# Normalising three of four token groups ahead, inside the stage before, in a one-core Trainium2 kernel of eight layers

## The chip, the cores and the metric

The kernel runs on one core of one Trainium2 chip. The time is device microseconds (us) of one execution, the median of several. The profiled execution is one of its own, and its span runs from the first to the last instruction of the core.

## The reference

2048 tokens (2 sequences of 1024) of 256 numbers pass four layers, each an attention and a feed-forward part with a residual, gated by tanh of an input. Nearly every part begins with the same layer norm over the 256 numbers of a token:

```
def _layernorm(x, axis=-1, eps=1e-05):
    m = jnp.mean(x, axis=axis, keepdims=True)
    v = jnp.var(x, axis=axis, keepdims=True)
    return (x - m) / jnp.sqrt(v + eps)
```

The parts, in order: joint attention (L0x), an 8-expert feed-forward (L0f), cross attention on 154 context tokens with a second norm of its own, with gain and shift (L1x), a routed feed-forward with 16 experts and 2 shared (L1f), linear attention (L2x), two local transformer layers (L2a0, L2f0, L2a1, L2f1), a feed-forward whose weights are the context (L3c) and a quantised feed-forward (L3f).

## The kernel before, in words

The tokens lie in SBUF as `x[128 partitions, T=16 tiles, 256]`. Four tiles are a group (G=4 groups, GT=4 tiles, GN=512 tokens). Stages are written as blocks: each engine (TensorE `tensor`, VectorE `vector`, ScalarE `scalar`, GpSimd `gpsimd`, SyncE `sync`) has its own list of instructions, ordered by semaphores, and all meet at a block's end; `net.reclaim()` clears semaphores and adds a barrier. `Weights(..)` with `load` is a block of its own in which SyncE issues the transfer; `w.need()` is another, in which SyncE waits until it has landed.

The norm between two stages is the block `layer_norm`. VectorE writes variance plus eps (L142 or L144), ScalarE takes the root (L174), VectorE the reciprocal (L147) and minus mean times reciprocal (L149), and the 16 tiles are normalised into `xn`: 13 by VectorE (L152), 3 by ScalarE (L170); with no transposed output it is 8 and 8. TensorE transposes them into 8 PSUM banks, four 128x128 blocks each (L163), and ScalarE alone brings the banks into `xT` (L189, or L191 with gain and shift). The mean and variance come from the stage before: `RowStats.take` does `bn_stats` (L96) for some tiles and then `bn_aggr` (L99). `root_table` (L104) loads ScalarE's table for the root early.

The norms that matter here, by the time of their first instruction: 681 us (inside cross attention, after its block of keys and values), 987 us (into L1f), 1343 us (into L2x), 1435 us (into the local layers, output by token, no transposes) and 2241 us (into L3c). Those at 12, 533 and 2293 us are left as they are.

Around them:

- The block of keys and values of `cross_attention`. GpSimd issues 16 gathers (indirect DMAs, L1720) that add the experts' results to `x`, then computes the rest of `wq` (L211) and `gated_bias` (L1725). VectorE evicts keys and values (value items 2, 3, 6 and 7 are the tails, four copies each, L1741), computes the rest of `wo` (L211, 128x2048, both operands in SBUF), and takes the statistics of a group once its gathers have landed.
- The main block of `cross_attention`. After its last unit TensorE projects group 3, VectorE adds it to `x` (L2023), then takes the last two statistics.
- `feed_forward`, for L1f and L2f1. Units `i = g*U + u`; TensorE does `up(i+2)`, then `down_mm(i)`. ScalarE applies the activation (L356) and splits weights three units ahead (L341); VectorE forms the hidden values (L432, L440, L429) and splits them (L206, L211); GpSimd computes the weights' rest. At `u == 0` of the next group VectorE runs `take(g-1)`: adds the result to `x` (L403, for L2f1 also L415) and takes the group's statistics. `up(i+2)` waits for `act_done` and `banks_read` of unit i, `down_mm(i)` for `hidden_ready`.
- `linear_attention`: eight steps of two tiles; `add_y` (L1193) and the statistics of two tiles follow three steps behind, the last two after the loop.

## Time and profile before

| | |
|---|---|
| median of 3 runs | 2498.22 us (2495.98 to 2506.04) |
| profiled execution | 2497.99 us |
| its span | 2495.7 us |
| TensorE busy | 2052.7 us, 82% of the span |
| VectorE busy | 1759.9 us, 71% |
| ScalarE busy | 1327.8 us, 53% |
| GpSimd busy | 1045.6 us, 42% |
| mean granted TensorE clock | 0.905 |

PE is TensorE's matmul, PEld its weight load, DVE VectorE, ACT ScalarE, POOL GpSimd, SP SyncE; a q behind a name is the engine's sequencer. In a timeline row stand the start in us, the time of the group in us, the engine, the line, the operation, output<-input with a shape, the count, and in brackets the idle time before it and what ended it. Instructions on DVE and ACT overlap by some 0.09 us, so the time of a group of n is less than n times one.

### The profile page before, as it was taken

What the parts mean: (1) busy time and instruction counts of PE and PEld (TensorE: products, weight loads), DVE (VectorE), ACT (ScalarE), POOL (GpSimd) and SP (SyncE); (2) the same over time, 40 slices, a digit from 0 to 9 for tenths busy, and PEclk for the clock granted to TensorE, in tenths of its full rate; (3) what the DMA queues carried; (4) which work ended last, traced back from release to release, by engine and by line L of the source; (5) the groups of instructions that cost most, each with busy time, mean ns of one, the idle gap of its engine ahead of it and who ended that gap; (6) DMA issues with size and microseconds to landing.
All of it is one profiled execution on the core that took longest, in us unless ns stands there. A gap on an engine that the chain in (4) does not pass through costs nothing. (4 is left out here: it accounts for less than half of the span.)

```text
span 2495.7 us, 41249 instructions
## 1 busy us (share of the span) xinstructions
PE 2052.7 (82%) x14744; PEld 1486.0 (60%) x14744; DVE 1759.9 (71%) x3778; ACT 1327.8 (53%) x3064; POOL 1045.6 (42%) x1053
## 2 busy tenths in 40 slices
PE   6899999966589997799997879886998886985254
PEld 5444444456556665688886668675877775764122
DVE  6899999855655554776765676766666675668896
ACT  4488888834354443333332247473436564323797
POOL 1333233115543431455553654543535452422554
PEclk9899999988799998899998989998998988987586
DMA  4244344154300001100002000002000001000000
GB/s 110 33 55 50 48 54 54 23 217 126 57 1 1 1 1 81 51 1 1 1 1 87 1 1 2 1 2 95 1 1 1 1 1 38 1 35 25 0 1 34
DMA packets 29257, 80.81 MB, mean 32 GB/s; under 512 B 6016, under 2 KB 20096, under 8 KB 27392
## 3 DMA queue, kind: packets, MB, share of 16 engines
q0 software_dynamic: 11136, 22.38, 7.2%
q1 hardware_dynamic: 17920, 55.80, 6.5%
q8 instruction: 120, 1.97, 0.3%
q14 instruction: 81, 0.66, 0.1%
HBM read 45.07 MB, written 12.06 MB: 23 GB/s over the span
## 5 line engine op out<-in xcount | busy, mean ns | idle before, releaser
L3028 ACT ACTIVATE probs<-psum 128x512 f32<-128x512 f32 (+1 forms) x640 | 344.0, 601 | 91.7 <-PE psum L2952 76.4
L3070 DVE TENSOR_REDUCE max_parts<-psum 128x1 f32<-128x512 f32 x512 | 320.1, 685 | 26.3 <-PE psum L2890 20.5
L199 PE MATMUL psum<-x_upper,weights_upper 128*128 128x512 f32 (+2 forms) x556 | 220.8, 397 | 27.5 <-POOL weights_rest L211 12.9
L211 POOL TENSOR_TENSOR weights_rest<-L1f,weights_upper 128x256 fp32r<-128x256 f32 x216 | 179.6, 858 | 147.9 <-ACT weights_upper L341 147.9
L2952 PE MATMUL psum<-q_stack,k_stack 50*128 50x512 f32 (+1 forms) x640 | 235.4, 453 | 0.2 <-ACT probs L3028 0.2
L199 PE MATMUL psum<-x_rest,weights_upper 128*128 128x512 f32 (+2 forms) x556 | 217.4, 391 | 0.0
L199 PE MATMUL psum<-x_upper,weights_rest 128*128 128x512 f32 (+2 forms) x556 | 216.3, 389 | 0.0
L2890 PE MATMUL psum<-k_stack,q_stack 48*128 48x512 f32 x512 | 192.6, 465 | 12.5 <-ACT probs L3028 7.8
L2962 PE MATMUL psum<-probs,v_tok 128*17 128x256 f32 x2560 | 194.7, 386 | 0.2 <-ACT probs L3028 0.2
L199 PE MATMUL psum<-weights_upper,hidden_upper 128*128 128x256 f32 (+1 forms) x572 | 178.2, 312 | 5.2 <-DVE hidden_rest L211 2.7
L2526 POOL TENSOR_TENSOR probs<-probs,row_sum 128x1024 f32<-128x1024 f32 x64 | 121.0, 1894 | 138.5 <-DVE row_sum L2545 138.5
L211 POOL TENSOR_TENSOR weights_rest<-L2f,weights_upper 128x256 fp32r<-128x256 f32 (+1 forms) x144 | 104.6, 755 | 163.1 <-ACT weights_upper L341 163.1
L199 PE MATMUL psum<-weights_upper,hidden_rest 128*128 128x256 f32 (+1 forms) x572 | 163.2, 285 | 0.0
L199 PE MATMUL psum<-weights_rest,hidden_upper 128*128 128x256 f32 (+1 forms) x572 | 163.0, 285 | 0.0
L2890 PEld LDWEIGHTS psum<-k_stack,q_stack 48*128 48x128 f32 x512 | 79.9, 189 | 124.2 <-DVE max_parts L3070 72.4
L2494 ACT ACTIVATE probs<-probs,row_least 128x256 f32<-128x256 f32 x256 | 126.9, 498 | 40.4 <-DVE row_least L2539 40.4
L2653 POOL DMA_DIRECT2D q_stack<-q_parts x56 | 30.5, 544 | 264.2 <-PE psum L2952 264.2
L199 PEld LDWEIGHTS psum<-x_upper,weights_upper 128*128 128x128 f32 (+1 forms) x556 | 105.9, 190 | 51.9 <-issue 24.4
L1934 ACT ACTIVATE L1x<-psum,row_least 128x154 f32<-128x154 f32 x256 | 95.4, 399 | 76.5 <-DVE row_least L1989 76.5
L1971 POOL TENSOR_TENSOR L1x<-L1x,row_sum 128x512 f32<-128x512 f32 x64 | 67.7, 1058 | 160.5 <-DVE row_sum L1994 160.2
L211 DVE TENSOR_TENSOR hidden_rest<-hidden,hidden_upper 128x512 fp32r<-128x512 f32 (+1 forms) x143 | 129.2, 903 | 4.9
L2391 POOL TENSOR_TENSOR cos_part<-cos_part,sin_part 128x1024 f32<-128x1024 f32 x32 | 76.5, 2389 | 116.0 <-DVE sin_part L2358 116.0
(515 smaller groups left out, 6035.0 us busy)
## 6 DMA issues: line engine op xcount, KB each, us to landing
k_stack<-k_parts POOLq DMA_DIRECT2D x56, 147.2 KB, 3.8
L1f<-in_L1f SPq DMA_DIRECT2D x1, 6016.0 KB
L2f<-in_L2f SPq DMA_DIRECT2D x2, 2268.0 KB, 9.8
L1x<-in_L1x SPq DMA_DIRECT2D x1, 4226.0 KB
k_stack<-k_parts POOLq DMA_DIRECT2D x56, 73.6 KB, 4.1
L0f<-in_L0f SPq DMA_DIRECT2D x1, 4096.0 KB, 12.3
L2a<-in_L2a SPq DMA_DIRECT2D x2, 2048.0 KB, 11.4
slots_x<-zeros SPq DMA_DIRECT2D x1, 3840.0 KB, 13.3
```

The costliest lines, as they stand in the source:

```text
L199: ins = pe.matmul(out, lhsT(a).bitcast(F32R), rhs(b).bitcast(F32R), start=start and n == 0, stop=stop and n == len(PASSES) - 1, skip_group ...
L211: return engine.tensor_tensor(dst.bitcast(F32R), src, up_part, ALU.subtract)
L1934: ins = act.activation(ex[:, n % NE, h, :], net.ps[:, SLOT + 2 * s + e, a * SC:(a + 1) * SC], ACT.Exp, bias=mn[:, s, e, a:a + 1], scale=-1 ...
L1971: pool.tensor_tensor(main, ex[:, n % NE, :, 0:P], spread(sm[:, n % NE, :], P), ALU.mult)
L2391: pool.tensor_tensor(cp, cp, s_part[:, t % NSP].rearrange("p a n -> p (a n)"), ALU.add).then_inc(added, 1)
L2494: ins = act.activation(pb[:, n % NPB, h, :], pb[:, n % NPB, h, :], ACT.Exp, bias=mn[:, n % NPB, h:h + 1], scale=-1.0, accum_out=sm[:, n % ...
L2526: pool.tensor_tensor(pb[:, n % NPB], pb[:, n % NPB], spread(sm[:, n % NPB, :], 2 * P), ALU.mult)\
L2890: ins = pe.matmul(out, qs[s][r, a * P:(a + 1) * P].bitcast(F32R), ks[s][r, k * 512:(k + 1) * 512].bitcast(F32R), start=True, stop=True)
L2952: pe.matmul(net.ps[0:m, ST + n % NS, :], ks[s][r, k * P:k * P + m].bitcast(F32R), qs[s][r, :].bitcast(F32R), start=True, stop=True).then_i ...
L2962: ins = pe.matmul(net.ps[32 * j:32 * j + HD + 1, PVB, 0:256], vt[:, b, k, h, :], pb[:, n % NPB, j * 256:(j + 1) * 256], start=k == 0, stop ...
L3028: act.activation(pb[0:m, n % NPB, (1 - e) * 512:(2 - e) * 512], net.ps[0:m, ST + (2 * n + e) % NS, :], ACT.Exp, scale=HD ** -0.5)\
L3070: ins = v.tensor_reduce(mx3[:, u % 2, a + 4 * e, k:k + 1], src, AX.X, ALU.max)
```

## The change

A new class `NormAhead` holds the pieces of a norm. Its buffers for variance plus eps, root, reciprocal and minus mean times reciprocal are now lasting, one set for all. For the five norms named above, the stage before runs these pieces for groups 0 to 2, and a new block `norm_end` does group 3, and the transposes of all four.

- One lasting buffer `nT` [128, 2, 2048] takes the place of the separate `xT`s. A normalised tile t is written at `nT[:, :, t*128:(t+1)*128]`; its two 128x128 blocks are transposed through PSUM back to the same places. (Into the local layers and L3c the tiles go to `y` by token.) `nT` and `y` also serve as other stages' scratch buffers.
- `norm_end`: VectorE takes group 3's statistics, spread, reciprocal, and normalises 3 tiles (ScalarE 1); without transposes 2 and 2. TensorE transposes groups 0 to 2 from the block's start, and group 3 once all is normalised. ScalarE evicts banks 0, 1, then does the root, then 2, its tile, 3, 4, 5 and 7; VectorE evicts bank 6.
- Keys and values: ScalarE takes the four tail items (16 copies) and normalises 12 tiles; VectorE takes statistics, spread and reciprocals by group, and the rest of `wq` and `gated_bias` from GpSimd. The block ends with VectorE's wait for the last gathers.
- Cross attention, end: the last two statistics leave; after those of groups 0 to 2 come settle and spread at unit U, then reciprocals and four tiles on VectorE before the last `add_y`s; ScalarE does the root and eight tiles at its end.
- Feed-forward L1f and L2f1: for each of the first three groups VectorE adds settle and spread to `take`, and reciprocals at `u == 2`; ScalarE adds the root at `u == 2` and four tiles at `u == 3`. The last `take` makes no statistics.
- Linear attention: the last two statistics leave; after the loop VectorE does spread, reciprocals and four tiles before the last two `add_y`s, ScalarE the root and eight tiles at its end. `norm_end` stands ahead of the reclaim.

```
+class NormAhead:
+    def spread(self, v, lo, hi):
+        r = self.net.rows
+        if self.again:
+            ins = v.tensor_scalar(r.ve[:, lo:hi], r.mv[:, lo:hi, 1], 1.0 + EPS, EPS * EPS, ALU.mult, ALU.add)
+        else:
+            ins = v.tensor_scalar(r.ve[:, lo:hi], r.mv[:, lo:hi, 1], EPS, None, ALU.add)
+        ins.then_inc(self.var_ready, 1)
+    def root(self, act, part, lo, hi):
+        r = self.net.rows
+        act.wait_ge(self.var_ready, part + 1)
+        act.activation(r.sd[:, lo:hi], r.ve[:, lo:hi], ACT.Sqrt).then_inc(self.sd_ready, 1)
+    def invert(self, v, part, lo, hi):
+        r = self.net.rows
+        v.wait_ge(self.sd_ready, part + 1)
+        v.reciprocal(r.rs[:, lo:hi], r.sd[:, lo:hi]).then_inc(self.rs_ready, 1)
+        v.wait_ge(self.rs_ready, part + 1)
+        v.scalar_tensor_tensor(r.nb[:, lo:hi], r.mv[:, lo:hi, 0], -1.0, r.rs[:, lo:hi], ALU.mult, ALU.mult)\
+            .then_inc(self.rows_ready, 1)
...
+def norm_end(net, ahead, parts, turns=None, xT=None, gain=None, shift=None, after=None):
+    LO = T - GT
+    OWN, OTHER = [(LO, LO + 1, LO + 2), (LO + 3,)] if turns else [(LO, LO + 1), (LO + 2, LO + 3)]
+    BY_VECTOR = (G - 1) * C
...
+        def _(v):
+            net.rows.take(v, step, ahead.src, range(LO, T))
+            step.settle()
+            ahead.spread(v, LO, T)
+            ahead.invert(v, parts, LO, T)
+            ahead.vector(v, OWN)
+            if turns:
+                v.wait_ge(early, BY_VECTOR + 1)
...
+            def _(pe):
+                for n in range(G * C):
+                    g, c = divmod(n, C)
+                    if n == BY_VECTOR:
+                        pe.wait_ge(ahead.normed, T)
+                    for t in range(g * GT, (g + 1) * GT):
+                        ins = pe.transpose(net.ps[:, n, t % GT * P:(t % GT + 1) * P], turns(t, c), net.ident[:])
+                    ins.then_inc(early, 1)
...
+            if turns:
+                take(0)
+                take(1)
+            ahead.root(act, parts, LO, T)
+            if turns:
+                take(2)
+            ahead.scalar(act, parts, OTHER)
+            if turns:
+                for n in range(3, G * C):
+                    if n != BY_VECTOR:
+                        take(n)
```

In `feed_forward`, on ScalarE and on VectorE:

```
+                if ahead is not None and g >= 1 and u == 2:
+                    ahead.root(act, g - 1, (g - 1) * GT, g * GT)
+                if ahead is not None and g >= 1 and u == 3:
+                    ahead.scalar(act, g - 1, range((g - 1) * GT, g * GT))
...
+                if ahead is not None and g == G - 1:
+                    return
                 net.rows.take(v, step, y if then is None else x, range(g * GT, (g + 1) * GT))
+                if ahead is not None:
+                    step.settle()
+                    ahead.spread(v, g * GT, (g + 1) * GT)
...
+                if ahead is not None and g >= 1 and u == 2:
+                    ahead.invert(v, g - 1, (g - 1) * GT, g * GT)
```

In the block of keys and values (GpSimd, then VectorE):

```
-                pool.wait_ge(wq_upper, 1)
-                rest(pool, wq[1][:], w("wq"), wq[0][:])
-                pool.tensor_scalar(gbo[:], w("bo"), factor, None, ALU.mult)
...
+                value(0)
+                value(1)
+                rows_of(0)
+                v.wait_ge(wo_upper, 1)
+                rest(v, wo[1][:], w("wo"), wo[0][:])
+                ahead.invert(v, 0, 0, GT)
+                value(4)
+                value(5)
+                v.wait_ge(wq_upper, 1)
+                rest(v, wq[1][:], w("wq"), wq[0][:])
+                v.tensor_scalar(gbo[:], w("bo"), factor, None, ALU.mult)
+                rows_of(1)
+                ahead.invert(v, 1, GT, 2 * GT)
+                rows_of(2)
+                ahead.invert(v, 2, 2 * GT, 3 * GT)
+                v.wait_ge(gathered[G - 1], 16 * GT)
```

In `linear_attention`, on ScalarE and on VectorE:

```
+            ahead.root(act, 0, 0, T - GT)
+            ahead.scalar(act, 0, range(GT, T - GT))
...
+            step.settle()
+            ahead.spread(v, 0, T - GT)
+            ahead.invert(v, 0, 0, T - GT)
+            ahead.vector(v, range(GT))
             for k in (PAIRS - 2, PAIRS - 1):
                 add_y(k)
-                statistics(k)
```

## Rows read from the trace of the kernel before

**Rows 1.** The page: busy time, share of the span and instructions of each engine

```profile
PE 2052.7 (82%) x14744; PEld 1486.0 (60%) x14744; DVE 1759.9 (71%) x3778; ACT 1327.8 (53%) x3064; POOL 1045.6 (42%) x1053
```

**Rows 2.** Stretches: busy us (instructions) of each engine, granted clock, DMA share, GB/s

```profile
676.50:690.90 14.40, 5.33 (x32) 5.09 (x32) 6.57 (x24) 7.58 (x13) 3.14 (x3) 0.64 0.00 0
982.70:996.40 13.70, 5.92 (x32) 5.69 (x32) 6.58 (x24) 6.23 (x12) 0.00 (x0) 0.63 0.76 310
1338.30:1352.30 14.00, 5.48 (x32) 5.24 (x32) 6.59 (x24) 6.11 (x12) 0.00 (x0) 0.63 0.72 284
1427.30:1440.30 13.00, 2.66 (x13) 1.89 (x13) 6.69 (x21) 4.84 (x10) 0.71 (x1) 0.77 0.00 1
...
1040.00:1100.00 60.00, 60.00 (x344) 50.84 (x344) 40.78 (x56) 21.66 (x53) 35.39 (x42) 1.00 0.00 1
```

**Rows 3.** Timeline of VectorE, from the end of L1f into the norm at 1343 us

```profile
1338.30 1.41 DVE L96 BATCH_NORM_STATS2 row_stats<-x_tok 128x6 f32<-128x256 f32 x4
1339.74 0.38 DVE L99 BATCH_NORM_AGGREGATE mean_var<-row_stats 128x2 f32<-128x6 f32 x4
1343.16 0.18 DVE L144 TENSOR_SCALAR var_eps<-mean_var 128x16 f32<-128x16 f32 x1 [3.04 <-PEq L3360]
...
1344.00 4.29 DVE L152 TENSOR_SCALAR xn<-x_tok,mean_var,rstd 128x256 f32<-128x256 f32 x13
```

**Rows 4.** Timeline of ScalarE in the norm at 1343 us

```profile
1343.37 0.22 ACT L174 ACTIVATE sd<-var_eps 128x16 f32<-128x16 f32 x1 [8.70 <-DVE var_eps L144]
1344.12 1.58 ACT L170 ACTIVATE xn<-x_tok,minus_mean_rstd,rstd 128x256 f32<-128x256 f32 x3 [0.53 <-DVE minus_mean_rstd L149]
1346.58 0.58 ACT L189 COPY xT<-psum 128x512 f32<-128x512 f32 x1 [0.88 <-PE psum L163]
...
1349.14 2.55 ACT L189 COPY xT<-psum 128x512 f32<-128x512 f32 x5 [0.27 <-PE psum L163]
```

**Rows 5.** Timeline of VectorE, keys and values, into the norm at 681 us

```profile
657.52 2.28 DVE L211 TENSOR_TENSOR wo_rest<-L1x,wo_upper 128x2048 fp32r<-128x2048 f32 x1
...
676.48 1.41 DVE L96 BATCH_NORM_STATS2 row_stats<-x_tok 128x6 f32<-128x256 f32 x4 [3.36 <-DMA x_tok<-slots_y,slots]
...
681.27 0.17 DVE L142 TENSOR_SCALAR var_eps<-mean_var 128x16 f32<-128x16 f32 x1 [2.98 <-PEq L1647]
```

**Rows 6.** Timeline of GpSimd, keys and values: gathers and what follows them

```profile
655.82 1.54 POOL L1720 DMA_INDIRECT x_tok<-slots_y,slots  x1 [0.30 <-issue]
657.66 3.56 POOL L1720 DMA_INDIRECT x_tok<-slots_y,slots  x1 [0.30 <-issue]
...
678.10 1.52 POOL L1725 TENSOR_SCALAR gated_bias<-L1x,cross_factor 128x256 f32<-128x256 f32 x1
```

**Rows 7.** Timeline of ScalarE in the norm at 681 us: evictions with gain and shift

```profile
684.70 5.93 ACT L191 ACTIVATE xT<-psum,L1x 128x512 f32<-128x512 f32 x8 [0.88 <-PE psum L163]
```

**Rows 8.** Timeline of ScalarE, from linear attention into the norm at 1435 us

```profile
1428.76 0.59 ACT L1058 COPY oT<-psum 128x512 f32<-128x512 f32 x1 [2.91 <-PE psum L983]
...
1435.94 4.04 ACT L170 ACTIVATE y_tok<-x_tok,minus_mean_rstd,rstd 128x256 f32<-128x256 f32 x8 [0.53 <-DVE minus_mean_rstd L149]
```

**Rows 9.** Timeline of VectorE, from linear attention into the norm at 1435 us

```profile
1433.00 0.25 DVE L99 BATCH_NORM_AGGREGATE mean_var<-row_stats 128x2 f32<-128x6 f32 x2
```

**Rows 10.** Timeline of ScalarE in L1f: two units, and the table load behind its last

```profile
1116.87 0.60 ACT L356 ACTIVATE activated<-psum 128x512 f32<-128x512 f32 x1 [1.96 <-PE psum L293]
1118.30 1.02 ACT L341 CAST weights_upper<-L1f 128x256 fp32r<-128x256 f32 x3 [0.83 <-PE psum L199]
1121.28 0.60 ACT L356 ACTIVATE activated<-psum 128x512 f32<-128x512 f32 x1 [1.96 <-PE psum L293]
...
1333.17 1.28 ACT L104 ACT_TABLE_LOAD   x1
```

**Rows 11.** Timeline of VectorE in L1f: the end of the same unit's hidden values

```profile
1118.22 0.69 DVE L440 TENSOR_TENSOR hidden<-product,psum 128x512 f32<-128x512 f32 x1
```

**Rows 12.** Timeline of TensorE in L2f1: its stall behind a group's take

```profile
2158.41 0.47 PE L199 MATMUL psum<-x_upper,weights_upper 128*128 128x512 f32 x1 [1.61 <-DVE hidden L429]
```

More of the change, by code:

```diff
@@ L1627, in three, with cross_attention @@
     return ins
-def cross_attention(net, x, factor, w, slots, slots_y, scale):
+def cross_attention(net, x, factor, w, slots, slots_y, nT, ahead, then):
     nc = net.nc
@@ L1958, in _ @@
                             take_q(u + 1, d)
-                net.rows.root_table(act)
+                then.root(act, 0, 0, T - GT)
+                then.scalar(act, 0, range(GT, T - GT))
             @block.gpsimd
@@ L2058, in _ @@
                                 rows_of(k)
+                        if u == U and d == 1:
+                            step.settle()
+                            then.spread(v, 0, T - GT)
                         if n < U * GT:
@@ L2576, in _, with local_attention @@
                     add_y(t - 2)
[L2579 removed]
+def local_attention(net, y, lw, nT):
     HD = LH * LD
```

200 lines of the change are left out of this document (135 added, 65 removed).

## The prediction, made before the change was run

> **What bounds the kernel now.** I read the page first: TensorE is busy 82% of the span and no engine comes near it [rows 1]. So the kernel is TensorE's work plus the places where TensorE has none. The table of stretches shows both kinds. Inside a feed-forward, 60 us hold 60 us of TensorE at the full clock (the last row of [rows 2]); nothing put on another engine costs time there while TensorE does not wait for it. From the last result of a stage to the first instruction of the next, where the norm stands, TensorE works 5.3 to 5.9 of some 14 us [rows 2]. There are five such places in the change: 14.4, 13.7, 14.0, 13.0 and, at 2236 us, 13.9 us (same pattern as the one at 1338). The timelines of the norm at 1343 us say what ends each step. VectorE's statistics of the last group take 1.82 us (start of L96 to end of L99), 3.04 us of block ends, SyncE's transfer block and reclaim follow, 13 tiles take 4.29 us, or 0.33 us each [rows 3]. ScalarE sees its first bank 3.42 us after the norm's first instruction (1346.58 less 1343.16), then one bank per 0.85 us for four banks, which is TensorE's pace at 1.2 GHz (the granted clock averages 0.63 over the stretch, [rows 2]), and after that its own pace, 2.55 us for five [rows 4]. The norm ends at 1351.69, 8.53 us after its start.
>
> **The change, norm by norm.** First the new block, `norm_end`, with transposes, counted from its start, since it is used four times. TensorE begins at 0 instead of 2.3 us. From TensorE's start to ScalarE's first bank it took 1.15 us, so bank 0 is there at 1.15, bank 1 at 2.0, bank 2 at 2.85, bank 3 at 3.7, banks 4 and 5 at 4.1 to 4.6 as the clock rises. VectorE: statistics 1.82, spread 0.18, so variance at 2.02; ScalarE's root waits behind bank 1 and ends at 2.7 (0.22, [rows 4]); reciprocal and product, 0.5 us, at 3.2; three tiles at 0.33 plus the tail of the last, 4.3. ScalarE: bank 2 until 3.44, one tile (0.58) until 3.95, banks 3, 4, 5 at 0.52 each until 5.5. TensorE's last two banks follow at 4.85 and 5.3; VectorE takes one (0.7, until 5.6), ScalarE the last until 6.0. I take 6.0 us, 6.2 where the clock rose one bank later (the norm at 987 us had five slow banks, 8.92 us in all). Bounds: 5.4 (the clock high after three banks) and 7.7 (it stays low: 1.15 and seven times 0.85, plus 0.58).
>
> - **Into L1f** (987 us). Before: 13.7 us from the last add to the next stage. After: block ends and transfers 2.7, `norm_end` 6.2, 0.26 to the next block, and 0.2 for the settle and spread that now stand ahead of VectorE's last splits of `oT`, for which TensorE waits: 9.4. **Gain 4.35.** ScalarE's eight tiles (4.04 us for eight, [rows 8]) lie beside TensorE's last projection, for which VectorE's last adds wait anyway, as do VectorE's four (1.35). The stage's weights are issued 1.9 us earlier too, so they stay as far ahead.
> - **Into L2x** (1343 us). Before 14.0, after 3.04 + 6.0 + 0.63 (the `need` block) = 9.65: gain 4.35. In the loop of L1f the spread costs 0.2 us of VectorE in each of three takes. There the hidden values of the next unit are already late (TensorE waits 0.3 us for them three times), so I charge all: 0.6. **Gain 3.75.** Bounds for one spread: 0 (VectorE catches up before TensorE asks) and 0.3.
> - **Into L3c** (2241 us). Same sum, before 13.85, after 2.9 + 6.0 + 0.6; TensorE stalls 1.61 us behind L2f1's take [rows 12], so three spreads again cost 0.6. **Gain 3.75.**
> - **ScalarE in both feed-forwards.** Per group: table load 1.28 [rows 10], root 0.22, load back 1.28, four tiles 2.2: 5.0 us. Cover: activations are 4.41 us apart and hold 1.62 of ScalarE's work [rows 10]. `up(i+2)` needs unit i's banks read. It starts one pitch and one `down` after the activation's start, 4.41 + 1.43 (ScalarE's wait at 1118.30 ends with that `down`) = 5.84 us; VectorE is done at 2.04 (1118.91 less 1116.87, [rows 10, 11]). Slack 3.8 us. The load back, if it stands behind the wait for TensorE, delays one activation by 1.3 us, the tiles the next by about 0.8 to 1.3; then it is made up. VectorE's reciprocals (0.5) fall in the same unit. I cost it at 0; uncovered it is the rival below. Late next would be `hidden_ready`, with even more slack.
> - **Into the cross attention** (681 us). Before: 14.4 us from the landing of the last gathers, 676.48 [rows 5], to the next stage. The block's end was set not by the statistics (678.3) but by GpSimd: `gated_bias` ends at 679.62, and VectorE restarts at 681.27 [rows 5, 6], 1.65 later. Both go. A plain block end elsewhere costs 0.3 us (ScalarE's last tile ends at 1439.98, the next stage starts at 1440.3, [rows 2, 8]), so the new one lies between 0.3 and 1.65; I take 1.0. Evictions here take 0.74 each (5.93 for eight, [rows 7]), and ScalarE, with seven of them, a root and a tile, is `norm_end`'s bound: 7.1. After: 1.0 + 7.1 + 0.26 = 8.4, a gain of 6.0. ScalarE's added work (16 tail copies, 12 tiles, three roots, about 11 us) begins at 659.7 and ends, by its waits for statistics, near 674.6, 2 us ahead of the landing. Against it, the gathers. One of the 16 took 3.56 instead of 1.54 us; it was issued 0.14 us after VectorE's `wo_rest` began, and 1.54 back from its end is 659.7, where `wo_rest` ends (659.80) [rows 5, 6]. A second such operation of 2.28 us, `wq_rest`, now runs among gathers 1.85 us apart. Each of the two holds a gather by 0.4 (issued just before it) to 2.3 us: 0.8 to 4.6 for both against 2.0 now. The middle, 2.7, is 0.7 worse. **Gain 5.3**, bounds 3.6 less 0.65 for the block end and 7.2 plus 0.7.
> - **Into the local layers** (1435 us). VectorE ended this stage at 1433.25 [rows 9]; without its last statistics it would end a microsecond earlier. But ScalarE's root now follows its last copy, which ends at 1429.35 [rows 8]; reciprocals by 1430.05, and then eight tiles, 4.04 us [rows 8], until 1434.1. So the stage ends 0.85 later. `norm_end` without transposes: 2.0 + 0.8, two tiles, 4.0, against 5.0 before; block ends are the same 2.1 us in sum. **Gain 0.2**, bounds -0.7 and 1.
>
> Sum: 4.35 + 3.75 + 3.75 + 5.3 + 0.2 = 17.35 us. Against the profiled execution's own 2497.99 that gives 2480.6; it lies 0.2 below the median of 2498.22, so the same number serves for both.
>
> The row of the slow gather meets a rule of the Trainium skill. Its page "SBUF — State Buffer", section "Who interferes with whom", says that a VectorE operation with two SBUF inputs blocks only GpSimd operations that read SBUF, and that descriptor generation, which writes, was not stalled by it (inferred there). By that rule `wq_rest` would cost the gathers nothing and the 3.56 us would have another cause that stays; the fourth term would be 6.0 and the time 2479.9. The row, whose end fits to a tenth, weighs more with me.
>
> **The rivals.** *One: ScalarE's added work in the feed-forwards reaches TensorE (slower).* Its place is units 2 and 3 of each later group in L1f and L2f1; from 3.8 us of delay on one activation it decides. If the delays do not overlap anything, six groups cost 5.0 each, 30 us: 2497.99 - 17.35 + 30 = 2510.6. For it: two table loads stand in the way of an activation, twice three times. Against it: the slack, and 21.66 of 60 us busy [rows 2]. 0.05.
>
> *Two: `norm_end` is hardly shorter than the norm (no change to speak of).* If TensorE's clock stays at 1.2 GHz, because it waits in the middle for group 3, or if ScalarE's order (root behind bank 1) drags, the block takes 7.7 us: 1.6 less four times, 6.4: 2487.0. For it: the low clock over the first four banks [rows 4]. Against: TensorE has six banks without a wait, longer than it took for the rise before. 0.17.
>
> *Three: the work ahead ends late, so that the stages end later and nothing is hidden.* In the keys and values block both VectorE operations hold a gather in full and ScalarE overruns: the term falls from 5.3 to 2.5; linear attention loses 0.7 instead of winning 0.2: 2484.3. It stays on the faster side. 0.15 of the 0.78 below.
>
> **How the numbers follow.** What a measurement of this kernel can tell from no change is 0.5%, 12.5 us. Forecast with rival three: 0.78. Rival two at 2487 would lie within 0.5% (2485.7 is the border): 0.17. Rival one: 0.05. Some of the forecast's own spread crosses the border (about 0.03) and some of rival two's falls short of it (0.02), so: faster 0.77, same 0.18, slower 0.05. Range: downwards the good bounds, gathers and block end 2.6, four `norm_end`s 0.5 each, spreads 1.2, of which all together are unlikely: 2475. Upwards rival two and some of the bad bounds at once: 2490. Slower than that, with rival one, is left out.
>
> **What would show it.** Right: the five stretches of [rows 2] measure 9.4, 9.65, 9.5, 9.1 (from the landing) and 12.8 us; in `norm_end` ScalarE's first eviction starts 1.15 us after the block's start; TensorE in units 2 to 4 of a later group waits for nothing new; the last gather lands between 675.5 and 679 on the old scale. Wrong: a wait of TensorE for ScalarE's activation in L1f or L2f1; ScalarE, not the gathers, ending the keys and values block; a `norm_end` of over 7 us without gain and shift; a gain in linear attention of over 1 us.

## The result and the profile after

The changed kernel takes 2483.85 us (median; 2472.17 to 2487.58) against 2498.30 us of the kernel before on the same chip: a ratio of 0.9925, 95% interval 0.9904 to 0.9945. In a later session its times gave 0.9937 (0.9918 to 0.9955). The forecast was 2480.6 us, which is 0.9929. One execution that took 3926.76 us is left out as disturbed. The times of both kernels spread from run to run, over 10 us before and 15 us after, and fall as the mean granted clock rises (2487.58 at 0.906, 2472.17 at 0.912), so single totals tell little here; stretches inside one profile tell more.

The page of the changed kernel, first part, answers to [rows 1]:

```profile
span 2485.6 us, 41328 instructions
## 1 busy us (share of the span) xinstructions
PE 2058.2 (83%) x14744; PEld 1488.5 (60%) x14744; DVE 1751.4 (70%) x3763; ACT 1366.2 (55%) x3137; POOL 1041.8 (42%) x1051
```

ScalarE gained 38 us of work and VectorE lost 8.5; neither tells where the time went. The table of stretches does. It runs from the end of VectorE's last instruction ahead of the norm to the first instruction of the next stage, and its last row is the same 60 us of a feed-forward as in [rows 2]. Columns: length, then busy time of PE, PEld, DVE, ACT, POOL with counts, granted clock, DMA share, GB/s.

```profile
678.55:691.59 13.04, 6.35 (x32) 6.14 (x32) 4.08 (x16) 7.82 (x13) 2.09 (x3) 0.57 0.18 26
986.22:995.19 8.97, 5.35 (x32) 5.15 (x32) 3.96 (x16) 4.45 (x9) 0.00 (x1) 0.81 0.79 303
1338.01:1347.96 9.95, 5.35 (x32) 5.14 (x32) 3.96 (x15) 4.40 (x9) 0.00 (x1) 0.83 0.76 289
1428.18:1436.06 7.88, 0.03 (x1) 0.06 (x1) 2.94 (x13) 2.76 (x6) 0.00 (x0) 0.64 0.00 1
2232.67:2243.07 10.40, 5.19 (x32) 4.77 (x32) 3.96 (x16) 4.30 (x9) 0.00 (x0) 0.68 0.70 274
1040.00:1100.00 60.00, 60.00 (x344) 50.81 (x344) 41.86 (x58) 22.49 (x56) 34.26 (x41) 1.00 0.00 1
```

TensorE makes the same 32 transposes in the three norms between stages (the second, third and fifth row) in 5.2 to 5.4 us, where it took 5.5 to 5.9 at a lower granted clock, but the stretches around them are 9 to 10.4 us long instead of 13.7 to 14.1 [rows 2]. Inside a feed-forward TensorE is still busy throughout.

Now the norm at 1341 us, VectorE's timeline and then ScalarE's, which answer to [rows 3] and [rows 4]:

```profile
1341.36 1.41 DVE L98 BATCH_NORM_STATS2 row_stats<-x_tok 128x6 f32<-128x256 f32 x4 [3.35 <-PEq L3538]
...
1343.21 0.17 DVE L211 TENSOR_SCALAR rows_var_eps<-mean_var 128x4 f32<-128x4 f32 x1
...
1346.31 0.69 DVE L283 COPY norm_turned<-psum 128x512 f32<-128x512 f32 x1 [1.10 <-PE psum L296]
```

```profile
1342.28 0.59 ACT L305 COPY norm_turned<-psum 128x512 f32<-128x512 f32 x1 [7.87 <-PE psum L296]
...
1346.74 0.59 ACT L305 COPY norm_turned<-psum 128x512 f32<-128x512 f32 x1 [0.22 <-PE psum L296]
```

The reader is to see three things. ScalarE's first eviction starts 0.92 us after the block does (I had 1.15; it is 1.12 at 684 and 2237 us and 0.66 at 989), while VectorE is still at its statistics. The last eviction ends at 1347.33, 5.97 us after the start, where I had 6.0. And the 3.35 us ahead of the block, ended by TensorE's sequencer, were 3.04 in [rows 3]: they grew by 0.31. At 2236 us the same idle time grew by over 1 us, and there the reason first looked hidden:

```profile
2236.58 1.41 DVE L98 BATCH_NORM_STATS2 row_stats<-x_tok 128x6 f32<-128x256 f32 x4 [3.91 <-PEq L3593]
```

In the keys and values (VectorE, then GpSimd; compare [rows 5, 6]) a gather beside each of the two subtractions of 128x2048 takes longer than the usual 1.54 us, the first by 2.11, the second by 0.34:

```profile
665.77 2.28 DVE L340 TENSOR_TENSOR wo_rest<-L1x,wo_upper 128x2048 fp32r<-128x2048 f32 x1
...
669.79 2.31 DVE L340 TENSOR_TENSOR wq_rest<-L1x,wq_upper 128x2048 fp32r<-128x2048 f32 x1
...
684.16 1.41 DVE L98 BATCH_NORM_STATS2 row_stats<-x_tok 128x6 f32<-128x256 f32 x4 [5.60 <-PEq L1791]
```

```profile
665.82 3.65 POOL L1885 DMA_INDIRECT x_tok<-slots_y,slots  x1 [0.30 <-issue]
669.78 1.55 POOL L1885 DMA_INDIRECT x_tok<-slots_y,slots  x1 [0.30 <-issue]
671.63 1.89 POOL L1885 DMA_INDIRECT x_tok<-slots_y,slots  x1 [0.30 <-issue]
...
679.38 1.55 POOL L1885 DMA_INDIRECT x_tok<-slots_y,slots  x1 [0.30 <-issue]
```

Keys, values and norm together, from ScalarE's first instruction in that block to the next stage, took 49.41 us before and take 43.80 now.

What eats part of the gain lies mostly where nothing was changed: up to the keys and values the profiled execution is 6.3 us later than before, with a granted clock in the first 200 us of 0.84 and 0.97 where it was 0.88 and 1.00. Such a difference comes and goes between executions: in the other profiles, whose code there is that of the changed kernel, the keys and values begin between 641.6 and 648.7 us (641.5 in the one profile before the change). One place looked like a price of the change. At the end of the cross attention TensorE waits 3.33 us for VectorE's last `oT_rest` (1.49 before), and the projection behind it takes 1.5 us longer:

```profile
972.20 0.36 PE L1769 MATMUL psum<-wo_upper,oT_upper 128*128 128x256 f32 x1 [3.33 <-DVE oT_rest L340]
```

### The profile page after: what moved, and what is told of

Same layout as the page of the kernel before. It is cut to its first block and busy times, and to the rows that moved or that the text cites. A ratio compares the mean times of both kernels' runs of the same rounds, so it can differ in the third digit from the quotient of the medians.

```text
span 2485.6 us, 41328 instructions
## 1 busy us (share of the span) xinstructions
PE 2058.2 (83%) x14744; PEld 1488.5 (60%) x14744; DVE 1751.4 (70%) x3763; ACT 1366.2 (55%) x3137; POOL 1041.8 (42%) x1051
## 6 DMA issues: line engine op xcount, KB each, us to landing
L1f<-in_L1f SPq DMA_DIRECT2D x1, 6016.0 KB, 22.2
```

## The experiments

All are edits of the changed kernel. Where only one execution was made, the verdict is read from stretches of its profile.

**late_turns.** Are the early transposes the gain, or the smaller number of tiles?

```diff
-                    if n == BY_VECTOR:
+                    if n == 0:
                         pe.wait_ge(ahead.normed, T)
...
-                take(0)
-                take(1)
             ahead.root(act, parts, LO, T)
-            if turns:
-                take(2)
             ahead.scalar(act, parts, OTHER)
             if turns:
-                for n in range(3, G * C):
+                for n in range(G * C):
```

> Edit of the changed kernel: in norm_end TensorE waits for all sixteen tiles before its first transpose, and ScalarE makes its root and its tiles of the last group first and evicts banks after; what is normalised ahead stays. If, as in my sum, the gain of norm_end comes from early transposes, TensorE begins 4 us after the block's start instead of at 0 and the eight banks then take what they took before the change (5.1 us from the first eviction to the end at 1343 us): norm_end 9 to 10.2 us instead of 5.9 to 6.1, +3 to +4 in each of four places, 2484 + 14 = 2498, about the time before the change. Rival: the gain comes from having only four tiles to normalise, the early transposes being bound by the low clock: under +1 in each place, 2484 to 2488.

2496.07 us, ratio to the kernel before 0.9991 (0.9977 to 1.0005): the whole gain is gone. VectorE's and ScalarE's rows of the norm, now at 1342.68:

```profile
1345.27 1.05 DVE L234 TENSOR_SCALAR norm_turned<-x_tok,mean_var,rows_rstd 128x256 f32<-128x256 f32 x3
```

```profile
1347.53 0.59 ACT L305 COPY norm_turned<-psum 128x512 f32<-128x512 f32 x1 [1.54 <-PE psum L296]
...
1351.81 0.59 ACT L305 COPY norm_turned<-psum 128x512 f32<-128x512 f32 x1 [0.18 <-PE psum L296]
```

The first eviction stands 4.85 us after the block's start instead of 0.92, the end 9.72 instead of 5.97. The four stretches grow by 3.2, 4.1, 3.7 and 5.1 us. Counted from VectorE's last add of the stage before, the four tiles with late transposes are hardly ahead of the sixteen of the old norm: 13.04 us instead of 13.75 into L1f, 13.69 instead of 14.06 into L2x, and 15.53 instead of 13.88 into L3c. So normalising twelve tiles ahead would be worth next to nothing by itself: the eight evictions, paced by TensorE's transposes, are what must be started early.

**pool_wq.** The subtraction for `wq` and `gated_bias` back on GpSimd.

```diff
             def _(pool):
...
+                pool.wait_ge(wq_upper, 1)
+                rest(pool, wq[1][:], w("wq"), wq[0][:])
+                pool.tensor_scalar(gbo[:], w("bo"), factor, None, ALU.mult)
...
-                v.wait_ge(wq_upper, 1)
-                rest(v, wq[1][:], w("wq"), wq[0][:])
-                v.tensor_scalar(gbo[:], w("bo"), factor, None, ALU.mult)
```

> Edit of the changed kernel: wq_rest and gated_bias go back to GpSimd, behind its gathers. My theory: the block of keys and values then ends by GpSimd again. Before the change gated_bias ended 7.0 us after the start of the last gather's issue and VectorE began again 1.65 us later; now the last issue starts at 679.4, 0.3 earlier without the hold beside wq_rest: VectorE restarts at 687.7 instead of 684.2, so the stretch of keys, values and norm is 43.8 + 3.5 = 47.3 us. And only one gather, the one beside wo_rest, is held (3.6 us), all others take 1.54 to 1.55. Rival: the block's end is set by the landing of the last gather and the barrier alone, since the restart now also comes 3.2 us behind the last issue; then the stretch stays within 0.5 us of 43.8.

GpSimd's last work and VectorE's restart:

```profile
674.15 1.55 POOL L1885 DMA_INDIRECT x_tok<-slots_y,slots  x1 [0.30 <-issue]
675.13 5.10 POOL L340 TENSOR_TENSOR wq_rest<-L1x,wq_upper 128x2048 fp32r<-128x2048 f32 x1
679.61 1.53 POOL L1890 TENSOR_SCALAR gated_bias<-L1x,cross_factor 128x256 f32<-128x256 f32 x1
```

```profile
682.79 1.41 DVE L98 BATCH_NORM_STATS2 row_stats<-x_tok 128x6 f32<-128x256 f32 x4 [9.47 <-PEq L1791]
```

From the start of the last issue to the restart it is 8.64 us instead of 4.78, and the restart comes 39.87 us after the block's first instruction instead of 36.37: +3.5, as expected. Keys, values and norm together take 46.91 us instead of 43.80, where 47.3 was expected, because the norm's end behind them took 6.77 us here and 7.16 there. (The single total, 2474.55 us, is lower than the changed kernel's; its cross attention ran at a granted clock of 0.99 instead of 0.96.) Only the gather beside `wo_rest` is held.

**split_rest.** Does VectorE's subtraction hold the gathers?

```diff
-                rest(v, wo[1][:], w("wo"), wo[0][:])
+                in_pieces(v, wo, "wo")
...
+                    for i in range(4):
+                        rest(v, *[ap[:, i * 512:(i + 1) * 512] for ap in flat])
```

(`flat` holds the three operands as 128x2048; the same for `wq`.)

> Edit of the changed kernel: wo_rest and wq_rest, 128x2048 each, are made in four operations of 128x512 each; nothing else changes. Now one gather beside wo_rest (2.28 us) takes 3.65 us and one beside wq_rest (2.31 us) 1.89, where the others take 1.54 to 1.55: 2.45 us of holds. Theory: a VectorE operation with two SBUF inputs holds the generation of descriptors until it ends; then each hold is at most one piece, 0.6 us, and both together come to 0 to 1.2 us. Rival one: the port is held as long as such operations follow each other, and the holds stay at 2 to 4 us. Rival two, by the Trainium skill, page SBUF - State Buffer, section Who interferes with whom: the generation is not stalled by such an operation; then the 3.65 us have another cause and stay at their place in the order of gathers.

```profile
666.68 2.49 DVE L340 TENSOR_TENSOR wo_rest<-L1x,wo_upper 128x512 fp32r<-128x512 f32 x4
...
670.69 2.49 DVE L340 TENSOR_TENSOR wq_rest<-L1x,wq_upper 128x512 fp32r<-128x512 f32 x4
```

```profile
666.74 2.04 POOL L1885 DMA_INDIRECT x_tok<-slots_y,slots  x1 [0.30 <-issue]
...
670.93 1.86 POOL L1885 DMA_INDIRECT x_tok<-slots_y,slots  x1 [0.30 <-issue]
```

The first gather is issued 0.06 us behind the start of the first piece and takes 0.50 us more than 1.54, not 2.11; the second is held 0.31. In sum 0.8 instead of 2.45. The hold follows the length of the operation beside it, so the operation is its cause. Two gathers that every profile has fit too: those at 650.45 and 652.49 us of the changed kernel, issued beside `wk_rest` and `wv_rest` (two operations of 128x1024 each, 1.22 us), take 1.74 and 1.95 us: up to the end of the operation that runs when they are issued, and then the usual 1.54. The operation that follows does not hold them again. The Trainium skill, page "SBUF — State Buffer", section "Who interferes with whom", says that an operation with two SBUF inputs did not stall descriptor generation; this run differs, and decides. What the gather waits with (its indices are read from SBUF too) was not told apart.

**sems_early, few_reclaims, barrier_only.** What grew ahead of the norms by 0.31 and 1.05 us? Between stages `reclaim` has GpSimd clear the semaphores of ended stages, one clear, with a drain of GpSimd ahead of it, for each contiguous run of ids, and then all engines meet. The norms' semaphores outlive their stage and cut these runs: in the built programs the nine reclaims make 1,3,4,4,6,4,7,6,6 clears before the change and 1,3,4,5,7,7,9,9,12 after it, 16 more. The first run takes those 25 semaphores at the start, the second leaves out six of nine reclaims, the third leaves them out but keeps their barrier.

```diff
+        held = [[net.sem(ctx, f"ahead{k}_{name}") for name in ("var", "sd", "rs", "rows", "normed")] for k in range(5)]
...
-        routed = NormAhead(net, into_routed, x, in_turned(nT))
+        routed = NormAhead(net, held[0], x, in_turned(nT))
```

```diff
-        net.reclaim()
+        pass
```

> Edit of the changed kernel: the 25 semaphores of the five norms made ahead are taken at the kernel's start and never given back, so that they don't cut the ranges of ids that the reclaims between stages clear: clears per reclaim fall from 1,3,4,5,7,7,9,9,12 to 1,3,4,3,7,4,8,6,9. Theory: GpSimd's clears stand on the path between stages at about 0.17 us each (six more clears cost 1.04 us in the idle time of VectorE ahead of the last feed-forward). Then that idle time falls from 3.91 to 3.4 us, the one into the linear attention from 3.35 to 3.0, twelve clears give 2.0 us in all. Rival: what grew there was something else (the block that holds the transfers, SyncE's queue): both idle times stay within 0.1 us.

> Edit of the changed kernel: six of the nine reclaims (the first, third, fourth, sixth, eighth and ninth) are left out, with their clears and their barrier; ids of stages that have ended are cleared together at the three that stay. Nothing of the computation changes. Theory: each clear left out on the path gives 0.17 us and each barrier 0.3 or so: VectorE's idle time into the last feed-forward falls from 3.91 to 1.6 us, into the linear attention from 3.35 to 2.2, into the routed feed-forward by 1.0; 38 clears less some that move to the three that stay, 5 us, and 2 us of barriers: 2477. Rival: the clears run beside other waits (block ends, the issue of transfers, the first loads) and the places shrink by the barrier at most: 2482 to 2484.

> Edit of the kernel with three reclaims: at the six places without one stands its barrier alone, without the clears. It parts the price of the clears from that of the barrier. From the runs so far: without reclaim VectorE's idle time ahead of the norm falls by 1.18 us (4 clears gone, into the routed feed-forward), 1.13 (5, into the linear attention) and 2.17 (12, into the last feed-forward), from which a clear is 0.15 us and a barrier 0.4 to 0.55. Theory: with the barrier these idle times are 2.0, 2.6 and 2.1 us (against 2.73, 3.35, 3.91 with clears and 1.55, 2.22, 1.74 with neither). Rival: the barrier is free behind the block's own end, and a clear costs 0.2 to 0.3: then they are within 0.1 us of 1.55, 2.22 and 1.74.

VectorE's idle times into L1f (the norm at 989 us), into the linear attention and into the last feed-forward, in brackets at the rows' ends. sems_early (the second and third):

```profile
1336.09 1.41 DVE L98 BATCH_NORM_STATS2 row_stats<-x_tok 128x6 f32<-128x256 f32 x4 [3.06 <-PEq L3538]
...
2228.11 1.41 DVE L98 BATCH_NORM_STATS2 row_stats<-x_tok 128x6 f32<-128x256 f32 x4 [3.43 <-PEq L3593]
```

and, in the same run, at the sixth and the eighth reclaim, both in the local layers:

```profile
1682.09 0.22 DVE L2307 MEMSET stats<- 128x192 f32 x1 [3.32 <-PEq L3564]
...
2079.46 0.22 DVE L2307 MEMSET stats<- 128x192 f32 x1 [2.64 <-PEq L3414]
```

few_reclaims:

```profile
980.56 1.40 DVE L98 BATCH_NORM_STATS2 row_stats<-x_tok 128x6 f32<-128x256 f32 x4 [1.55 <-PEq L3415]
...
1331.86 1.41 DVE L98 BATCH_NORM_STATS2 row_stats<-x_tok 128x6 f32<-128x256 f32 x4 [2.22 <-PEq L3538]
...
2218.60 1.41 DVE L98 BATCH_NORM_STATS2 row_stats<-x_tok 128x6 f32<-128x256 f32 x4 [1.74 <-PEq L3593]
```

barrier_only:

```profile
980.70 1.41 DVE L98 BATCH_NORM_STATS2 row_stats<-x_tok 128x6 f32<-128x256 f32 x4 [1.89 <-PEq L3415]
...
1332.19 1.41 DVE L98 BATCH_NORM_STATS2 row_stats<-x_tok 128x6 f32<-128x256 f32 x4 [2.55 <-PEq L3538]
...
2222.18 1.41 DVE L98 BATCH_NORM_STATS2 row_stats<-x_tok 128x6 f32<-128x256 f32 x4 [2.07 <-PEq L3593]
```

The theory holds, with a price that is not the same for each clear. In sems_early three clears fewer give 0.48 us into the last feed-forward (3.91 to 3.43) and two fewer 0.29 into the linear attention (3.35 to 3.06). In the local layers three fewer give 0.42 and 0.48 (3.74 to 3.32, 3.12 to 2.64) and one fewer 0.15 (2.11 to 1.96), which brings the first two back to what they were before the change (3.35 and 2.65); their clears are then as many as before, too. So a clear more or less is 0.14 to 0.16 us. One thing is left: into the linear attention the wait grew by 0.31 for a single clear more, and with one clear fewer than before the change it is still 3.06 against 3.04. Some 0.15 us there are not clears, and what they are is open.

The barrier costs 0.33 to 0.34 in the three places shown (1.89 less 1.55 and its two like) and at the first reclaim, but only 0.11 and 0.04 at the sixth and the eighth. The clears of one reclaim cost the rest: 0.51 us for a single one, 0.84 for 4, 0.80 for 5, 1.34 for 7, 1.67 for 9, 1.84 for 12. few_reclaims takes 2470.71 us, 0.9885 of the kernel before (0.9865 to 0.9905), against the 2477 expected. Its idle times at the reclaims are 8.4 us shorter in sum, with two more in the local layers falling from 3.74 to 2.29 us and from 3.12 to 1.41; the times say 10 (by the ratios) to 13 us, and what goes beyond 8.4 is not shown to come from the edit. sems_early came out at 2479.04, one execution.

**scalar_load.** How much slack has ScalarE in the two feed-forwards?

```diff
                     ahead.root(act, g - 1, (g - 1) * GT, g * GT)
+                    for _ in range(4 * g):
+                        load(act.copy(extra[:], y[:, 0:2, :].rearrange("p t d -> p (t d)")))
+                        load.settle()
```

> Edit of the changed kernel: in both feed-forwards that make the norm ahead, ScalarE makes 4, 8 and 12 further copies of 128x512 in the second, third and fourth group, right behind the root in the unit of number 2 (about 0.65 us each with its wait: 2.6, 5.2 and 7.8 us). It measures the slack that the prediction put at 3.8 us. Theory: a delay of ScalarE up to 3.8 us costs TensorE nothing and what is beyond it costs in full: the intervals between the takes in the routed feed-forward, 79.65, 79.64 and 73.71 us, grow by 0, 1.4 and 4.0; those in the feed-forward of the local layers likewise by 0 to 1, 1 to 2 and 4. Rival: the slack is used up by the work that is there; then they grow by 2.6, 5.2 and 7.8. If they grow by less than 1 in the third group, the slack was far larger than I took it.

ScalarE in the third and fourth group of L1f:

```profile
1183.85 5.17 ACT L497 COPY extra<-x_tok 128x512 f32<-128x512 f32 x8
...
1190.33 0.60 ACT L489 ACTIVATE activated<-psum 128x512 f32<-128x512 f32 x1
```

```profile
1265.27 7.77 ACT L497 COPY extra<-x_tok 128x512 f32<-128x512 f32 x12
...
1274.35 0.60 ACT L489 ACTIVATE activated<-psum 128x512 f32<-128x512 f32 x1
```

TensorE's waits behind them, which the changed kernel does not have:

```profile
1192.51 0.47 PE L328 MATMUL psum<-x_upper,weights_upper 128*128 128x512 f32 x1 [1.52 <-DVE hidden L585]
...
1276.53 0.47 PE L328 MATMUL psum<-x_upper,weights_upper 128*128 128x512 f32 x1 [4.13 <-DVE hidden L585]
```

The load is 2.56, 5.17 and 7.77 us. The activation behind it starts 10.72, 13.33 and 15.93 us after its group's take, where the changed kernel has 8.25: it is 2.47, 5.08 and 7.68 us later. The intervals between takes are 79.64, 81.42 and 79.68 us where they were 79.65, 79.64 and 73.71: +0, +1.8 and +6.0. A delay of 2.47 costs nothing; one of 5.08 costs 1.8, a slack of 3.3 us. The third would cost 4.4 by that slack and costs 6.0; there the granted clock is 0.83 from 1272 to 1280 us, around TensorE's stop of 4.13 us, while it stayed at 1.00 around the stop of 1.52. I put the slack at 3.8, counted from the moment the activation is due. Before the change it starts 7.96 us after the take, and VectorE's spread moves that by 0.2, so the changed kernel has used less than 0.1 of the slack: measured the same way it is 3.4, a little less than I put. In the local layers the intervals are 29.72, 31.46 and 29.40 us; 31.5 for the second comes up without the load too, and the last is 22.2 to 23.7 without it, so it costs 5.7 to 7.2 there and the slack is no larger than in L1f; how much smaller, these intervals do not part from the clock.

**spread_later.** Where do the 0.2 us of the spread go? (The spread is VectorE's variance plus eps, and the settle ahead of it its wait for its own statistics.)

```diff
                 net.rows.take(v, step, y if then is None else x, range(g * GT, (g + 1) * GT))
-                if ahead is not None:
-                    step.settle()
-                    ahead.spread(v, g * GT, (g + 1) * GT)
...
+                if ahead is not None and g >= 1 and u == 1:
+                    step.settle()
+                    ahead.spread(v, (g - 1) * GT, g * GT)
```

> Edit of the changed kernel: in the feed-forwards the settle and the spread stand one unit later on VectorE, behind the hidden values of unit 1 instead of inside the take. Theory of the prediction: the take of unit 0 is where VectorE is late, one unit on it has caught up, so the intervals between takes go back from 79.65, 79.64 and 73.71 to 79.44, 79.43 and 73.50, and TensorE's waits for hidden values from 1.7 to 1.0 us each. Rival: VectorE is still late in unit 1, and the same 0.2 us appears there: the intervals stay within 0.05.

The intervals between takes in L1f are 79.45, 79.43 and 73.49, those of the kernel before (79.44, 79.43, 73.48) to a hundredth. So 0.2 us at the take were 0.2 us of the kernel, three times, and cost nothing one unit later. (TensorE's waits for hidden values in L1f, at the takes only, are 0.34 us before the change, 0.56 with it and 0.34 here.) Total 2477.05, one execution.

**cross_end.** Is VectorE's share of the norm why TensorE waits 3.33 us?

```diff
                         if u == U + 1 and d == 0:
+                            for k in range(3, 6):
+                                rows_of(k)
+                            step.settle()
+                            then.spread(v, 0, T - GT)
                             then.invert(v, 0, 0, T - GT)
...
-                        if u == U:
-                            for k in range(3 * d, 3 * d + 3):
+                        if u == U and d == 0:
+                            for k in range(3):
                                 rows_of(k)
-                        if u == U and d == 1:
-                            step.settle()
-                            then.spread(v, 0, T - GT)
```

> Edit of the changed kernel: at the cross attention's end the last six tiles of the statistics and the spread stand behind VectorE's last rests of oT instead of ahead of them; the reciprocals and VectorE's four tiles follow at once. Theory: these statistics are why TensorE waits 3.33 us at 972 us for oT_rest instead of 1.49, and why its clock then falls: the wait returns to 1.5 us or less, and the stretch of the cross attention, 294.63 us, falls by 2 to 3. The norm's work still lies beside the last projection (VectorE 4.6 us, ScalarE 4.7 behind it, against two products of about 5 us each), so the norm behind it, 8.97 us, does not grow by more than 0.3. Rival: the statistics are not what oT_rest waits for (ScalarE's oT_upper is): wait and stretch stay, within 0.5 us, and the norm's share moves past the last add.

```profile
970.08 0.36 PE L1769 MATMUL psum<-wo_upper,oT_upper 128*128 128x256 f32 x1 [1.49 <-DVE oT_rest L340]
```

The wait falls to 1.49 us and the stretch from 294.63 to 291.28: expected 2 to 3 less, measured 3.35. But the other profiles forbid to charge this to the change. Here is TensorE over the 8 us ahead of that projection and over the projection, in the changed kernel, then in pool_wq, whose code is the same there, then before the change:

```profile
964.20:972.20 8.00, 3.65 (x17) 1.29 (x17) 7.75 (x30) 1.39 (x3) 0.00 (x0) 1.00 0.00 0
972.20:985.47 13.27, 13.23 (x96) 13.03 (x96) 2.21 (x6) 4.04 (x8) 0.00 (x0) 0.87 0.01 1
```

```profile
955.70:963.70 8.00, 5.23 (x16) 1.61 (x17) 7.75 (x30) 1.28 (x3) 0.00 (x0) 0.79 0.00 0
963.70:975.48 11.78, 11.74 (x96) 11.53 (x96) 2.22 (x7) 4.05 (x8) 0.00 (x0) 1.00 0.01 1
```

```profile
962.16:970.16 8.00, 5.35 (x17) 1.77 (x17) 7.64 (x28) 2.03 (x3) 0.00 (x0) 0.79 0.01 2
970.16:981.94 11.78, 11.74 (x96) 11.53 (x96) 0.75 (x2) 0.63 (x2) 0.00 (x0) 1.00 0.00 1
```

From VectorE's last copy ahead of it to the projection's start it is 7.76 to 7.77 us in all eleven profiles with the changed code, at either clock, and 7.63 before: the settle and the spread cost 0.13 us, not 1.84. In some executions the lower clock (0.79 over the stretch) falls on TensorE's products ahead of the wait, which hides it and leaves 1.5 to 1.75 us of waiting (seven of the eleven, and the one profile before the change); in others TensorE is through early, waits 3.33 and gets the lower clock in the projection, 1.5 us longer (the other four). Whether the change makes the second case more frequent, one profile of the kernel before can't tell. cross_end removes 1.83 us of VectorE's path in the second case and, as the combined kernel shows below, 0.13 in the first.

**linear_order.** What ends the linear attention?

```diff
                 if s == PAIRS:
                     net.rows.root_table(act)
-            ahead.root(act, 0, 0, T - GT)
-            ahead.scalar(act, 0, range(GT, T - GT))
+                    ahead.root(act, 0, 0, T - GT)
+            ahead.scalar(act, 0, range(2 * GT, T - GT))
...
-            ahead.vector(v, range(GT))
+            ahead.vector(v, range(2 * GT))
```

> Edit of the changed kernel, linear attention: ScalarE's root stands ahead of its last copy (oT) instead of behind it, VectorE normalises eight tiles and ScalarE four. My sum said that the root behind the last copy and ScalarE's eight tiles end this stage (here until 1429.64 us, while VectorE's last add ends at 1428.18 and waited 2.74 us for the root before). Theory: the stage then ends with VectorE's last add, its idle time of 1.77 us ahead of the norm's statistics falls to 0.3, and the time from the last add to the local layers from 7.88 to 6.4 us; the last add itself is not later. Rival: the idle time is block ends and not ScalarE, and stays; or the root ahead of the copy makes the copy late and the last add with it.

```profile
1411.68 1.64 DVE L1336 SCALAR_TENSOR_TENSOR x_tok<-psum,tanh_gates,x_tok 128x512 f32<-128x512 f32 x2
1413.64 1.41 DVE L98 BATCH_NORM_STATS2 row_stats<-x_tok 128x6 f32<-128x256 f32 x4 [0.32 <-PEq L1068]
```

The idle time is 0.32 us instead of 1.77, the way to the local layers 6.44 instead of 7.88, and the last add is 0.3 us earlier in its stage. The step that the prediction blamed for the term's smallness is the right one, and it can be had back: 1.8 us.

**combined and control.** Everything that helped, in one, beside the changed kernel itself. The one edit not shown yet:

```diff
                 take(0)
-                take(1)
             ahead.root(act, parts, LO, T)
             if turns:
+                take(1)
                 take(2)
```

> The changed kernel with what the runs so far found, in one: three reclaims instead of nine; wo_rest and wq_rest in four pieces each; the statistics at the cross attention's end behind the last rests of oT; spreads one unit later; the order of linear_order in the linear attention; and in each norm's end ScalarE's root ahead of its second bank. Sum of the places, against the changed kernel: reclaims 7 to 9 us, holds of the gathers 1.6, cross attention 1.8 to 3.4, spreads 1.2, linear attention 1.4, root 0.2 in each of four: 14 to 18 us, so 2466 to 2470, under both kernels. Rival: part of it is taken back by TensorE's clock, which is granted lower where TensorE waits less elsewhere; then 2472 or more.

> The changed kernel as it is, beside the combined one and the kernel before on the same chip, to put the sum of places against the times. If the prediction's sum of 17 us holds in the times it comes out at 0.993 of the kernel before; if the three places that measured worse than forecast count in full, 0.9945 or more. The combined kernel should stand 14 to 18 us below it.

control 2484.89 us, 0.9937 (0.9918 to 0.9955); combined 2472.99 us, 0.9890 (0.9874 to 0.9906), 11.9 us less. That is under both kernels, but short of the 14 to 18 expected, and not to be told from few_reclaims alone (0.9885): the times do not show that the other edits add anything. The five stretches around the norms are 1.3, 1.3, 1.0, 1.8 and 1.4 us shorter than in control and the cross attention 2.5. Against that L1f is 2.2 us longer: from its start to the first take 108.43 us at a mean clock of 0.92, where control had 105.56 at 0.94. That is not the edits' doing either: of the other profiles seven have 108.4 to 108.5, the rest lie between 106.2 and 109.2. The rival, that TensorE's clock takes part back, fits, and in one place it looks like more than chance: the block ahead of L3c takes 5.8 to 5.9 us in every profile with early transposes in which the idle time ahead of it is 3.4 us or more, and 6.33, 6.42 and 6.62 us in barrier_only, few_reclaims and combined, where that time is 2.07, 1.74 and 1.74. Its granted clock is 0.67, 0.66 and 0.64 there and 0.75 in control. The other norms show no such thing. The root ahead of the second bank shows no gain: from the block's start to the next stage it is 6.2 and 6.6 us at 984 and 1334 us, and 6.2 and 6.5 in control.

## Why the prediction was right

The sum of 17.35 us against the profiles, place by place (spreads and settles included; from stretches of the two profiled kernels, the 0.28 from control):

| place | forecast | measured | working |
|---|---|---|---|
| into L1f | 4.35 | 4.65 | 13.75 - 8.97 - 0.13 |
| into L2x | 3.75 | 3.46 | 14.06 - 9.95, less 3 spreads, 0.65 |
| into L3c | 3.75 | 3.20 | 13.88 - 10.40, less 0.28 |
| cross attention | 5.3 | 5.61 | 49.41 - 43.80 |
| local layers | 0.2 | -0.1 | 14.35 - 14.44, each from the start of the last `o_tok` |
| sum | 17.35 | 16.82 | |
| reclaims in the local layers | 0 | -1.2 | 0.39 + 0.31 + 0.47 |

15.7 us in all; the ratios times 2498.3 give 18.7 and 15.7. The forecast chose the right mechanism, and its 2480.6 lies between the two sessions (2479.6 and 2482.6). That it is so close is in part luck: the places miss by up to 0.6 us each way, 1.2 us were not in the sum at all, and single runs of the changed kernel spread over 15 us.

- **`norm_end`**: 6.0 to 6.2 us forecast, 5.97 measured at 1341 us, 5.98 at 988.96 and 5.85 at 2236.58; 7.16 with gain and shift (7.1). late_turns shows that it is the early start of the evictions, as the step had it. Rival two (7.7 us, the clock staying low) did not come in this profile, but nearly so in single places of others whose edits do not touch the block: 6.97 us in sems_early, 6.99 and 7.23 in scalar_load, 7.10 in split_rest, at a granted clock of 0.59 to 0.61 where the profiled kernel has 0.71.

```profile
1332.38:1339.50 7.12, 6.47 (x32) 6.23 (x32) 3.96 (x15) 4.59 (x9) 0.00 (x0) 0.60 0.98 406
```

(split_rest, from the block's start to just behind its end; columns as above.) Here rival two costs 1.1 us in one place; its 2487 needed 1.6 in all four at once.

- **ScalarE in the feed-forwards at nothing**: right. The slack was 3.4 us against 3.8. The load back does not stand behind the wait: at 2215.44 us it runs before the activation at 2217.04 is due, and in L1f it ends at 1111.84, within 0.1 us of when that activation is due. The longest delay seen, 0.8 us in the third group of L2f1 in control (the activation is 8.75 us behind the take, 7.93 before the change), is shorter than the 1.3 that I allowed for. TensorE has no wait in the two loops that it did not have before. Rival one is out.
- **Spreads**: 0.21 to 0.23 us each in L1f, as taken. In L2f1 the three cost 0.28 together (intervals of 29.72, 31.47 and 22.24 us in control, 29.49, 31.50 and 22.16 before), not 0.6. Here a term was mis-sized: TensorE waits for hidden values behind the first take (1.61 us before, 1.83 in control) and the second (0.97 and 0.95), and only the first wait grew. In the profiled kernel the second and third interval are 29.71 and 23.74 us; the clock moves 1.5 to 1.8 us from one to the other, so these two say nothing of the spreads.
- **Keys and values**: right in all parts. The last issue stands 4.78 us ahead of the restart, where landing (3.85 before) and block end (1.0) made 4.85; the gathers are held 2.45 us instead of 2.7. ScalarE's work ahead is done at 680.66, which on the old scale, 6.31 us earlier, is 674.35, where I had 674.6 and a landing 2 us behind it. Nothing of rival three came here.
- **Linear attention**: the step was named (root behind the last copy, eight tiles) and the size missed by 0.3. The stage ends 0.74 us later (0.85 forecast) and `norm_end` takes 3.80 us (4.0), but the block ends around it, put at the same 2.1 us, take 2.6; the reclaim behind them has seven clears instead of six, and the rest of that is open.
- **Missing from the working**: the clears of semaphores. The change adds 25 long-lived semaphores; I counted their waits and not what they do to `reclaim`. VectorE's idle times at the reclaims grew by 0.31 into L2x, 1.05 into L3c and 1.2 in the local layers, 2.5 us, the largest error of the sum. Fifteen of the 16 new clears stand there, 2.1 to 2.4 us at 0.14 to 0.16 each. The places into L1f and the cross attention gave 0.6 back.

## What to carry to other kernels

Where stages are parted by a serial piece (statistics, normalise, transpose, evict), ask which engine's chain sets its length and start that one first; here eight evictions paced by transposes, and making the tiles early without transposing them early gives nothing. Count what a change does to the housekeeping between stages: each run of semaphore ids to clear is an instruction on the path of all engines, and clearing only where ids run out took 8.4 us out of the idle times, half of what the change itself gave. Before a new wait in one profile is charged to a change, look at the same rows of other executions: the clock can move a wait of 1.8 us from one engine's account to another's.

## What the runs showed of the hardware beyond the expected

- Clearing one more contiguous run of semaphore ids on GpSimd (drain and clear) costs 0.14 to 0.16 us between stages, a single one by itself 0.51 and twelve 1.84; a further meeting of all engines costs 0.33 in four places and 0.04 and 0.11 in two.
- A VectorE subtraction with both inputs in SBUF holds a gather issued beside it until it ends: 2.11 us beside one of 2.28, 0.50 beside pieces of 0.62. The next such operation does not hold it again.
- A stop of TensorE of 4.13 us in a feed-forward went with a granted clock of 0.83 over the 8 us around it, and the interval grew by 6.0 us; one of 1.52 us left the clock at 1.00, and the interval grew by 1.8.
